# A transformer layer on one core: the order of the first batch's keys, values, norms and queries

## The chip, the core and the metric

The kernel runs on one core of a Trainium2 chip. A core has TensorE (PE in the rows; PEld is its loading of weights), VectorE (DVE), ScalarE (ACT), GpSimd (POOL), and SyncE (SP), which here issues most transfers. Each engine works through its own list of instructions in order; semaphores make one wait for another. The metric is the time of one execution on the device in microseconds (us), as the median of several runs; lower is better.

## The reference, cut to what matters

```python
# x: (16, 64, 512); ctx_1024: (16, 1601, 512); 16 heads of 32
def xattn(q, k, v, mask, w_q, w_k, w_v, w_o):
    query, key_, value = proj(q, w_q), proj(k, w_k), proj(v, w_v)      # (x @ w.T) by heads
    scores = einsum('bhqd,bhkd->bhqk', query, key_) / sqrt(32)
    scores = where(mask == 0, -1e9, scores)
    return merge(softmax(scores) @ value) @ w_o.T
x = x + xattn(layernorm(x), ctx_1024, ctx_1024, mask, w_q, w_k, w_v, w_o)
x = x + self_attention_with_lora(layernorm(x))
x = x + mixture_of_20_experts_top_2(layernorm(x))
```

The change concerns the beginning of the first line, the cross-attention.

## The kernel before

Context and keys. The kernel looks through the mask on the chip and finds which of five chunks of 400 context columns count; with these inputs one chunk does. So each of the 16 batches has 400 keys and values, which are computed from one piece of context of 128 x 4 x 400 numbers (800 KB; the 4 are slices `k` of the 512 features). Queries are computed once for all batches: 1024 rows of x, in two halves of 512 rows, four groups `m` of features each.

Precision. A matrix product of float32 data is made of three products (`mm3`, L186 to L190): each operand is split in a high part, copied by ACT to the type fp32r (`weight_hi`, `context`, `turn_x` in `scalar`), and a low part, source minus high part, by DVE (`rest`, L1084; `weight_lo`, `context`, `turn_x` in `vector`). A product can begin only when both parts of both operands are there. The helper line of every copy of ACT is L761, of every such subtraction L1084; of products L188 to L190, of transposes L194.

Stages. First the preamble, which the change reorders: load x in two halves, take its norms (`bn`, `variance`; POOL's `power` gives the inverse root), find the used chunks (`cm`, `fl`, `fr`, `frow`, `used`), normalise (`apply_x`, into `xn`, two buffers), transpose (`turn_x`, through banks 5 and 6 into `xt`, one buffer for both halves), queries (`queries(0)`, `queries(1)`, four products each), the keys of batch 0 (`k_part(0, g)`, four) and its values (`v_part(0, j)`, four). Then batches n = 0 to 15: `cross` writes each engine's order out by hand. For n it interleaves the transposes and value products of batch n - 1 (`t_part`, `pv_part`) with the keys of n (`k_part`), then scores (`s_part`, two halves) and values (`v_part`); DVE subtracts from the row's extreme, ACT exponentiates, POOL scales (L1637). Then the output projection, self-attention and the experts, which the change leaves as they are.

Order. PSUM banks 0 to 3 are given out in turn by the list `uses`; `freed` makes a product wait until the use four places before it has been read out. In the preamble PE's order is: transposes 0 to 3, two LoRA products, `queries(0)`, transposes 4 and 5, keys 0 and 1, transposes 6 and 7, keys 2 and 3, `queries(1)`; then `cross(0)` begins with scores and values of batch 0. SP issues in this order: constants, LoRA factors, first half of x, the mask rows (1 MB), the query weights `wq` (1 MB), the context of batch 0 once x is there, `wk` and the second half of x once the mask rows are there, mask and exclusions, and `wv` once DVE has split `wq` (both use `raw[:, 0]`). The next batch's context is issued when DVE has split the last one.

## Time and profile before

| | |
|---|---|
| time, median of 3 runs | 773.29 us (771.12 to 774.63) |
| span of the profiled execution | 772.6 us |
| busy share of the span | PE 92%, PEld 75%, DVE 53%, ACT 47%, POOL 37% |
| granted TensorE clock, mean | 0.960 of full speed |
| DMA | 74.77 MB |

The profile was taken in one execution. Of it the page gives the span, from the first instruction to the last, and no other time; the median of the runs is 0.7 us above this span. A busy share is an average over stages; the windows below tell them apart. In the page's second part the span is cut into 40 slices of 19.3 us, with the busy tenths of each. PE has 1 in the first slice and 9 in the next 30; DMA has 8 in the first slice, 4 in the second, and 0, 1 or 2 in the 29 after it.

### The profile page before, as it was taken

How to read it: one execution, taken by the hardware profiler on the slowest of the kernel's cores; microseconds unless marked ns; L12 is line 12 of the kernel's file. 1: busy time of each engine (PE TensorE's matmuls, PEld its weight loads, DVE VectorE, ACT ScalarE, POOL GpSimd, SP SyncE). 2: the span in 40 equal slices, each digit the busy share in tenths (PEclk: the TensorE clock that was granted, in tenths of full speed). 3: DMA queues.
4: the chain of work that ended last, by engine and by line, in shares of the span. 5: the costliest groups of instructions: out<-in, count | busy, mean ns of one | idle time of the engine just before them, and what ended most of it. 6: DMA issues, size and time to landing. Idle time of an engine off the chain costs nothing.

```text
span 772.6 us, 16928 instructions
## 1 busy us (share of the span) xinstructions
PE 708.0 (92%) x6817; PEld 581.6 (75%) x6817; DVE 410.2 (53%) x938; ACT 360.6 (47%) x665; POOL 289.0 (37%) x259
## 2 busy tenths in 40 slices
PE   1999999999999999999999999999999766999970
PEld 0787788778878887888788977887778554788860
DVE  5834434453344424533543345735368348799965
ACT  2425445453545345535454343533455431599950
POOL 0005135513553255225532453432225132788530
PEclk9999999999999999999999999999999985799995
DMA  8401101220021101110110002021001580999818
GB/s 294 149 1 43 45 2 45 98 91 24 29 98 44 44 2 44 44 39 7 44 44 2 3 3 75 1 79 45 3 29 57 188 303 21 330 394 397 333 52 326
DMA packets 30268, 74.77 MB, mean 97 GB/s; under 512 B 4053, under 2 KB 4437, under 8 KB 29155
## 3 DMA queue, kind: packets, MB, share of 16 engines
q1 hardware_dynamic: 25778, 65.16, 23.6%
q0 software_dynamic: 4400, 8.41, 2.9%
q8 instruction: 58, 0.95, 0.5%
q14 instruction: 32, 0.25, 0.1%
HBM read 66.13 MB, written 13.44 MB: 103 GB/s over the span
## 4 chain that ended last, share of the span: by engine, by line
PE 86%; DVE 6%; DMA 3%; ACT 2%; issue 2%; SPq 0%; POOL 0%; DVEq 0%; POOLq 0%; ACTq 0%
PE bank L188 22%; PE bank L190 21%; PE bank L189 20%; PE bank L194 10%; PE bank L345 4%; PE bank L322 3%; DMA raw<-in_wq 2%; DVE x_sb L1611 1%; PE bank L564 1%; DMA wr<-scratch_ys 1%; PE bank L551 1%; PE bank L665 1%; PE bank L580 1%; DVE wh L1084 1%; DVE stats L1340 0%
## 5 line engine op out<-in xcount | busy, mean ns | idle before, releaser
L1637 POOL TENSOR_SCALAR pp<-pp,rl 128x400 f32<-128x400 f32 x128 | 163.8, 1297 | 234.8 <-DVE rl L1162 234.8
L1217 DVE COPY pt<-bank 128x512 f32<-128x512 f32 x64 | 44.3, 692 | 99.4 <-PE bank L194 99.3
L188 PE MATMUL bank<-chi,wk 128*128 128x400 f32 x256 | 93.5, 365 | 0.0
L844 ACT ACTIVATE pp<-pp,acc 128x400 f32<-128x400 f32 x128 | 79.0, 619 | 28.0 <-DVE acc L1250 27.7
L1250 DVE CUSTOM_DVE_ANT_0 pp<-bank,cap 128x400 f32<-128x400 f32 x128 | 66.8, 569 | 46.5 <-PE bank L322 46.5
L190 PE MATMUL bank<-chi,wk 128*128 128x400 f32 x256 | 88.3, 345 | 0.0
L189 PE MATMUL bank<-clo,wk 128*128 128x400 f32 x256 | 88.3, 345 | 0.0
L188 PE MATMUL bank<-wv,chi 128*128 128x512 f32 x200 | 83.5, 417 | 0.0
L189 PE MATMUL bank<-wv,chi 128*128 128x512 f32 x200 | 78.5, 393 | 0.0
L190 PE MATMUL bank<-wv,clo 128*128 128x512 f32 x200 | 78.5, 392 | 0.0
L761 ACT ACTIVATE pt<-bank 128x512 f32<-128x512 f32 x64 | 38.2, 597 | 76.4 <-PE bank L194 75.3
L194 PE MATMUL bank<-cst,pp 128*128 128x128 f32 x512 | 67.2, 274 | 0.6 <-DVE x_sb L1194 0.6
L188 PE MATMUL bank<-wh,xu 128*128 128x512 f32 x152 | 65.8, 433 | 1.0 <-DVE xu L1084 0.7
L194 PEld LDWEIGHTS bank<-cst,pp 128*128 128x128 f32 x512 | 58.5, 140 | 5.8 <-issue 0.8
L190 PE MATMUL bank<-wh,xu 128*128 128x512 f32 x152 | 62.2, 409 | 0.0
L189 PE MATMUL bank<-wh,xu 128*128 128x512 f32 x152 | 61.8, 407 | 0.0
L761 ACT ACTIVATE vv<-bank 128x512 f32<-128x512 f32 x50 | 29.1, 583 | 65.0 <-PE bank L190 65.0
L188 PEld LDWEIGHTS bank<-wv,chi 128*128 128x128 f32 x200 | 37.5, 187 | 27.9 <-issue 19.4
L1149 DVE COPY kk<-bank 128x400 f32<-128x400 f32 x32 | 18.4, 575 | 61.9 <-PE bank L190 61.9
L189 PEld LDWEIGHTS bank<-clo,wk 128*128 128x128 f32 x256 | 48.3, 189 | 0.0
L188 PEld LDWEIGHTS bank<-chi,wk 128*128 128x128 f32 x256 | 48.2, 188 | 0.0
L190 PEld LDWEIGHTS bank<-chi,wk 128*128 128x128 f32 x256 | 48.1, 188 | 0.0
(238 smaller groups left out, 1387.4 us busy)
## 6 DMA issues: line engine op xcount, KB each, us to landing
wr<-in_We SPq DMA_DIRECT2D x13, 1024.0 KB, 11.6
craw<-in_ctx SPq DMA_DIRECT2D x16, 800.0 KB, 4.4
raw<-in_We SPq DMA_DIRECT2D x8, 1024.0 KB, 10.5
acc<-in_We SPq DMA_DIRECT2D x6, 1024.0 KB, 11.0
scratch_xn<-acc SPq DMA_DIRECT2D x16, 256.0 KB
wr<-scratch_ys SPq DMA_DIRECT2D x8, 512.0 KB, 7.2
x_sb<-in_x SPq DMA_DIRECT2D x2, 1024.0 KB, 8.5
out_dram<-x_sb SPq DMA_DIRECT2D x8, 256.0 KB, 5.9
```

Of the source, the lines that this page charges most:

```text
L188: pe.matmul(o, lhs[0], rhs[0], start=start, stop=False)
L189: pe.matmul(o, lhs[0], rhs[1], start=False, stop=False)
L190: return pe.matmul(o, lhs[1], rhs[0], start=False, stop=stop)
L194: last = pe.transpose(bank[0:n, k * 128:(k + 1) * 128], of(k), ident)
L322: last = pe.matmul(scores[64 * c:64 * c + 64, j, :], qc[r, 2 * half + c, 64 * b:64 * b + 64], kk[r, 2 * half + c, :], start=True, stop=True)
L345: last = pe.matmul(turned[32 * j:32 * j + 32, g, :], vv[:, (25 * (n // 8) + 3 * (n % 8) + i4) % 4, 128 * g + 32 * j:128 * g + 32 * j + 32] ...
L761: return act.activation(dst, src, ACT.Copy)
L844: act.activation(frame(p8), frame(p8), ACT.Exp, bias=bias, scale=-1.0, accum_out=total).then_inc(S["a_exp"], 1)
L1149: dve.tensor_copy(kk[:, g, :], at("k", 4 * n + g)[:, 0:CW]).then_inc(S["v_k"], 1)
L1217: dve.tensor_copy(pt[:, p8 % 4, :, :].rearrange("p a c -> p (a c)"), at("t", 8 * (n - 1) + p8)[:, :]).then_inc(S["v_pt"], 1)
L1250: dve.tensor_tensor_reduce(out=frame(p8), in0=scores[:, p8 % 4, :], in1=cap[:, :], scale=-1.0, scalar=nm[:, b, p8:p8 + 1] if seg else 3e38 ...
L1637: pool.tensor_scalar(frame(p8), frame(p8), rl[:, n % 2, p8:p8 + 1], None, ALU.mult).then_inc(S["g_pn"], 1)
```

## The change

The first context and `wk` are loaded in four pieces, one for each slice `k`, each with a semaphore of its own (`d_first`), ahead of everything but the constants; ACT and DVE split each piece as it comes (`first_keys`), and PE multiplies it for all four key groups, which stay open in banks 0 to 3. Then come three of the four values of batch 0, and only then the transposes of x and the queries, of which four are made between the scores of batch 0. `wq` now uses the slot of `wk`, is loaded when `wk` is split, and its low part is computed by POOL. All eight tiles of `xn` have their own place (in `acc`), and the second half of `xt` lies in `oh`, so the waits for a free buffer go. The LoRA products move to the start.

```diff
+        xn = acc[:, 0:8 * D].rearrange("p (i n) -> p i n", i=8)
...
-        xt = [sb(f"xt{j}", [128, 4, 512], f32r, first) for j in range(2)]
-        xn = sb("xn", [128, 2, D], f32, first)
+        xt = [[sb(f"xt{j}", [128, 4, 512], f32r, first) for j in range(2)], oh]
...
-        uses = [("q", m) for m in range(4)] + [("k", g) for g in range(4)] + [("q", 4 + m) for m in range(4)]
+        uses = [("k", g) for g in range(4)] + [("v", j) for j in range(3)] + [("q", m) for m in range(7)]
+        uses += [("v", 3), ("q", 7)]
...
+            def lora_products():
+                pe.wait_ge(S["d_cst"], 16)
+                pe.wait_ge(S["d_par"], 16)
+                for j in range(2):
+                    last = pe.matmul(pb[4][:, j * 128:(j + 1) * 128], lora[:, 2 * j, :], lora[:, 2 * j + 1, :],
+                                     start=True, stop=True)
+                last.then_inc(S["p_ids"], 1)
+
+            def first_keys():
+
+                c = columns(0)
+                for k in range(4):
+                    pe.wait_ge(S["v_w"], k + 1)
+                    for g in range(4):
+                        last = mm3(pe, at("k", g)[:, 0:CW], [w[:, k, g * 128:(g + 1) * 128] for w in wk],
+                                   [chi[:, k, c], clo[:, k, c]], k == 0, k == 3)
+                        if k == 3:
+                            last.then_inc(S["p_k"], 1)
+
+            def used_chunks():
+                pe.wait_ge(S["v_ids"], 3)
+                pe.transpose(pb[7][0:NC_, 0:128], fl[:, 0:NC_], ident).then_inc(S["p_ids"], 1)
+
+            def chunk_order():
+                pe.wait_ge(S["v_ids"], 4)
+                pe.matmul(pb[7][0:1, 0:10], fr[:, :], cst[0:NC_, 128:138], start=True, stop=True).then_inc(S["p_ids"], 1)
...
                 pe.wait_ge(S["v_xn"], i + 1)
-                if i >= 2:
-                    pe.wait_ge(S["v_xt"], i - 1)
-                turn4(pe, pb[5 + i % 2], lambda k: xn[:, i % 2, k * 128:(k + 1) * 128]).then_inc(S["p_xt"], 1)
-
-            def queries(hf):
-                pe.wait_ge(S["v_w"], 1)
+                if i >= 3:
+                    pe.wait_ge(S["v_xt"], i - 2)
+                elif i == 0:
+                    pe.wait_ge(S["v_ids"], 2)
+                turn4(pe, pb[4 + i % 3], lambda k: xn[:, i, k * 128:(k + 1) * 128]).then_inc(S["p_xt"], 1)
+
+            def queries(n):
+                hf, m = divmod(n, 4)
+                pe.wait_ge(S["g_h"], 1)
                 pe.wait_ge(S["v_xt"], 4 * hf + 4)
-                for m in range(4):
-                    for ready in freed("q", 4 * hf + m):
-                        pe.wait_ge(*ready)
-                    for k in range(4):
-                        last = mm3(pe, at("q", 4 * hf + m)[:, :], [w[:, k, m * 128:(m + 1) * 128] for w in wh[0]],
-                                   [v[:, k, :] for v in xt], k == 0, k == 3)
-                    last.then_inc(S["p_q"], 1)
+                for ready in freed("q", n):
+                    pe.wait_ge(*ready)
+                for k in range(4):
+                    last = mm3(pe, at("q", n)[:, :], [w[:, k, m * 128:(m + 1) * 128] for w in wh[0]],
+                               [v[:, k, :] for v in xt[hf]], k == 0, k == 3)
+                last.then_inc(S["p_q"], 1)
...
-                    if new:
...
+                    elif new:
+                        queries(4)
+                        s_part(0, 0)
+                        queries(5)
+                        s_part(0, 1)
+                        queries(6)
+                        v_part(0, 3)
+                        queries(7)
+
+            lora_products()
+            first_keys()
+            v_part(0, 0)
+            v_part(0, 1)
+            used_chunks()
+            for i in range(4):
+                turn_x(i)
+            v_part(0, 2)
+            chunk_order()
             queries(0)
-            turn_x(4)
-            turn_x(5)
-            k_part(0, 0)
-            k_part(0, 1)
-            turn_x(6)
+            queries(1)
+            for i in range(4, 7):
+                turn_x(i)
+            queries(2)
             turn_x(7)
-            k_part(0, 2)
-            k_part(0, 3)
-            queries(1)
-            pe.wait_ge(S["v_ids"], 5)
+            queries(3)
...
                 act.wait_ge(S["p_xt"], i + 1)
-                if i >= 4:
-                    act.wait_ge(S["p_q"], 4)
-                copy(xt[0][:, :, (i % 4) * 128:(i % 4 + 1) * 128], kview(pb[5 + i % 2])).then_inc(S["a_xt"], 1)
+                copy(xt[i // 4][0][:, :, (i % 4) * 128:(i % 4 + 1) * 128], kview(pb[4 + i % 3])).then_inc(S["a_xt"], 1)
+
+            def first_keys(k):
+                act.wait_ge(d_first[k], 32)
+                copy(chi[:, k, columns(0)], craw[:, k, :])
+                copy(wk[0][:, k, :], raw[:, 1, k, :]).then_inc(S["a_w"], 1)
+
+            def half_hi(dst, src, h):
+                copy(dst[0][:, 2 * h:2 * h + 2, :], src[:, 2 * h:2 * h + 2, :]).then_inc(S["a_w"], 1)
...
+            def value(n, j):
+                if j >= made(n + 1):
+                    return
+                act.wait_ge(S["p_v"], j + 1)
+                if n:
+                    act.wait_ge(S["p_pv"], 2 * n)
+                else:
+                    act.wait_ge(S["p_ids"], 1)
+                copy(vv[:, j % 4, :], at("v", j)[:, :]).then_inc(S["a_v"], 1)
...
                     for g in range(4):
-                        if g % 2 == 0:
-                            value(made(n) + g // 2)
+                        if not n:
+                            if g == 3:
+                                value(0, 3)
+                            else:
+                                queries(4 + g)
+                        elif g % 2 == 0:
+                            value(n, made(n) + g // 2)
...
+                    if n:
+                        value(n, made(n) + 2)
+                        value(n, made(n) + 3)
+                    else:
+                        queries(7)
...
-            weight_hi(wh[0], raw[:, 0], (d_raw[0], 16))
+            for k in range(4):
+                first_keys(k)
+            act.wait_ge(d_raw[0], 16)
+            half_hi(wv, raw[:, 0], 0)
+            half_hi(wv, raw[:, 0], 1)
+            k_part(0, 0)
+            k_part(0, 2)
+            act.wait_ge(d_raw[1], 16)
+            half_hi(wh[0], raw[:, 1], 0)
+            half_hi(wh[0], raw[:, 1], 1)
+            value(0, 0)
+            value(0, 1)
             for i in range(4):
                 turn_x(i)
-            context(0)
-            weight_hi(wk, raw[:, 1], (d_raw[1], 16))
-            weight_hi(wv, raw[:, 0], (d_raw[0], 32))
+            value(0, 2)
             queries(0)
+            context(1)
+            queries(1)
             turn_x(4)
             turn_x(5)
-            k_part(0, 0)
             turn_x(6)
+            queries(2)
             turn_x(7)
-            k_part(0, 2)
-            queries(1)
-            act.wait_ge(S["v_ids"], 5)
+            queries(3)
+            act.wait_ge(S["v_ids"], 7)
...
+            def first_keys(k):
+                dve.wait_ge(S["a_w"], k + 1)
+                c = columns(0)
+                ins = rest(clo[:, k, c], craw[:, k, :], chi[:, k, c])
+                if k == 3:
+                    ins.then_inc(S["v_ctx"], 1)
+                rest(wk[1][:, k, :], raw[:, 1, k, :], wk[0][:, k, :]).then_inc(S["v_w"], 1)
+
+            def first_values(h):
+                dve.wait_ge(S["a_w"], h + 5)
+                c = slice(2 * h, 2 * h + 2)
+                return rest(wv[1][:, c, :], raw[:, 0, c, :], wv[0][:, c, :])
...
-                if i >= 2:
-                    dve.wait_ge(S["p_xt"], i - 1)
-                norm(i, xn[:, i % 2, :]).then_inc(S["v_xn"], 1)
+                norm(i, xn[:, i, :]).then_inc(S["v_xn"], 1)
...
+                pv, c = kview(pb[4 + i % 3]), slice((i % 4) * 128, (i % 4 + 1) * 128)
+                rest(xt[i // 4][1][:, :, c], pv, xt[i // 4][0][:, :, c]).then_inc(S["v_xt"], 1)
...
-                    if b + 1 < NB:
+                        weight_lo(wh[0], raw[:, 0], 9)
+                    if n and b + 1 < NB:
                         context(n + 1)
...
-                            dve.wait_ge(S["p_q"], 8)
+                            dve.wait_ge(S["p_q"], 4)
...
-            dve.wait_ge(d_x[0], 16)
+            dve.wait_ge(S["p_ids"], 1)
+            for j in range(2):
+                own.on(dve.tensor_tensor(mbd[:, j, :], pb[4][:, j * 128:(j + 1) * 128], cst[:, 256:384], ALU.mult))
+            dve.wait_ge(own.sem, own.n)
+            for j in range(2):
+                dve.tensor_tensor(mbd[:, j, :], mbd[:, j, :], ident, ALU.add).then_inc(S["v_ids"], 1)
+            for k in range(4):
+                first_keys(k)
+            dve.wait_ge(S["d_x"], 16)
             for i in range(4):
                 own.on(bn(i))
             variance(0, 4)
+            first_values(0)
+            first_values(1).then_inc(S["v_w"], 1)
+            k_part(0, 1)
+            k_part(0, 3)
...
-            apply_x(0)
-            apply_x(1)
-            weight_lo(wh[0], raw[:, 0], 1)
-            dve.wait_ge(S["p_ids"], 1)
+            for i in range(4):
+                apply_x(i)
+            dve.wait_ge(S["p_ids"], 2)
             dve.tensor_reduce(fr[:, :], pb[7][0:NC_, 0:128], AX.X, ALU.max).then_inc(S["v_ids"], 1)
             for i in range(4):
                 turn_x(i)
-                if i < 2:
-                    apply_x(i + 2)
-                elif i == 2:
-                    dve.wait_ge(S["p_ids"], 2)
-                    dve.tensor_copy(frow[:, 0:10], pb[7][0:1, 0:10]).then_inc(S["v_ids"], 1)
-            context(0)
-            weight_lo(wk, raw[:, 1], 2)
-            dve.wait_ge(S["v_ids"], 3)
-            used()
-            dve.wait_ge(d_x[1], 16)
+            dve.wait_ge(S["d_x"], 32)
             for i in range(4, 8):
                 own.on(bn(i))
             variance(4, 4)
+            dve.wait_ge(S["p_ids"], 3)
+            dve.tensor_copy(frow[:, 0:10], pb[7][0:1, 0:10]).then_inc(S["v_ids"], 1)
             scaled(4, 4)
-            apply_x(4)
-            apply_x(5)
-            weight_lo(wv, raw[:, 0], 3)
+            for i in range(4, 8):
+                apply_x(i)
             make_cap(0)
-            dve.wait_ge(S["p_ids"], 3)
-            for j in range(2):
-                own.on(dve.tensor_tensor(mbd[:, j, :], pb[7][:, j * 128:(j + 1) * 128], cst[:, 256:384], ALU.mult))
-            dve.wait_ge(own.sem, own.n)
-            for j in range(2):
-                dve.tensor_tensor(mbd[:, j, :], mbd[:, j, :], ident, ALU.add).then_inc(S["v_lora"], 1)
-            turn_x(4)
-            apply_x(6)
-            turn_x(5)
-            apply_x(7)
-            k_part(0, 1)
-            turn_x(6)
-            turn_x(7)
-            k_part(0, 3)
             dve.wait_ge(S["v_ids"], 5)
+            used()
+            context(1)
+            for i in range(4, 8):
+                turn_x(i)
+            dve.wait_ge(S["v_ids"], 7)
...
+            for h in range(2):
+                pool.wait_ge(S["a_w"], 7 + h)
+                for k in (2 * h, 2 * h + 1):
+                    ins = pool.tensor_tensor(wh[0][1][:, k, :], raw[:, 1, k, :], wh[0][0][:, k, :].bitcast(f32),
+                                             ALU.subtract)
+            ins.then_inc(S["g_h"], 1)
             power(4, 4, (S["v_var"], 2), S["g_rstd"])
-            pool.wait_ge(S["p_q"], 8)
+            pool.wait_ge(S["p_q"], 4)
+            pool.wait_ge(S["v_xn"], 8)
+            pool.wait_ge(S["v_ids"], 7)
             alone(pool.memset(pp[:, 0:8 * D].rearrange("p (t c) -> p t c", t=8)[:, :, 0:PW], 0.0))
             alone(pool.memset(pp[:, 8 * D:8 * D + PW], 0.0))
...
+            for k in range(4):
+                sp.dma_start(craw[:, k, :], t["ctx"][0, 0, :, k, :]).then_inc(d_first[k], 16)
+                sp.dma_start(raw[:, 1, k, :], t["wk"][:, k, :]).then_inc(d_first[k], 16)
             xv = t["x"].rearrange("(i b) q d -> i (b q) d", b=2)
-            sp.dma_start(x_sb[:, 0:4, :], xv[0:4].rearrange("i p d -> p i d")).then_inc(d_x[0], 16)
+            sp.dma_start(x_sb[:, 0:4, :], xv[0:4].rearrange("i p d -> p i d")).then_inc(S["d_x"], 16)
+            sp.dma_start(raw[:, 0], t["wv"]).then_inc(d_raw[0], 16)
             for h in range(2):
                 sp.dma_start(mska[64 * h:64 * h + 64, :, :], t["rows"]).then_inc(S["d_cap"], 16)
-            sp.wait_ge(S["d_cst"], 16)
-            sp.dma_start(raw[:, 0], t["wq"]).then_inc(d_raw[0], 16)
-            sp.wait_ge(d_x[0], 16)
-            sp.dma_start(craw[:, :, :], t["ctx"][0, 0]).then_inc(S["d_ctx"], 16)
-            sp.wait_ge(S["d_cap"], 32)
-            sp.dma_start(raw[:, 1], t["wk"]).then_inc(d_raw[1], 16)
-            sp.dma_start(x_sb[:, 4:8, :], xv[4:8].rearrange("i p d -> p i d")).then_inc(d_x[1], 16)
+            sp.wait_ge(S["v_w"], 4)
+            sp.dma_start(raw[:, 1], t["wq"]).then_inc(d_raw[1], 16)
+            sp.wait_ge(S["d_x"], 16)
+            sp.dma_start(x_sb[:, 4:8, :], xv[4:8].rearrange("i p d -> p i d")).then_inc(S["d_x"], 16)
+            sp.wait_ge(S["v_ctx"], 1)
+            sp.dma_start(craw[:, :, :], t["ctx"][1, 0]).then_inc(S["d_ctx"], 16)
...
-                    context(16 * seg + b + 1, b + 1, chunk)
+                    if seg or b:
+                        context(16 * seg + b + 1, b + 1, chunk)
...
                     if seg == 0 and b == 5:
+                        sp.wait_ge(S["g_h"], 1)
...
+            sp.wait_ge(S["d_cap"], 32)
             for h in range(2):
                 sp.dma_start(mski[64 * h:64 * h + 64], t["mask"][0]).then_inc(S["d_cap"], 16)
             sp.dma_start(excl[:, :], t["excl"][0]).then_inc(S["d_cap"], 16)
-            sp.wait_ge(S["v_w"], 1)
-            sp.dma_start(raw[:, 0], t["wv"]).then_inc(d_raw[0], 16)
-            sp.wait_ge(S["v_ids"], 5)
+            sp.wait_ge(S["v_ids"], 7)
```

## Rows read from the trace of the kernel before

**Rows 1.** The chain that ended last, by engine (the page's part 4).

```profile
PE 86%; DVE 6%; DMA 3%; ACT 2%; issue 2%; SPq 0%; POOL 0%; DVEq 0%; POOLq 0%; ACTq 0%
```

**Rows 2.** Windows: us, busy time (count) by engine, TensorE clock, DMA share, GB/s.

```profile
24.50:72.40 47.90, 47.84 (x241) 39.02 (x241) 24.60 (x64) 20.38 (x38) 8.37 (x8) 1.00 0.11 37
...
175.00:470.00 295.00, 294.40 (x3246) 244.90 (x3245) 122.75 (x322) 130.75 (x297) 118.48 (x93) 1.00 0.09 30
```

**Rows 3.** Timeline of the start: start us, duration us, engine, line, out<-in.

```profile
9.01 0.69 DVE L1091 BATCH_NORM_STATS2 stats<-x_sb 128x6 f32<-128x512 f32 x1 [8.12 <-DMA x_sb<-in_x]
...
12.73 2.24 DVE L1270 TENSOR_REDUCE cm<-qc 128x5 f32<-128x2000 int32 x1 [0.23 <-DMA qc<-in_rows]
...
15.23 1.91 ACT L761 ACTIVATE wh<-raw 128x2048 fp32r<-128x2048 f32 x1 [13.20 <-DMA raw<-in_wq]
...
16.05 1.00 DVE L1100 TENSOR_SCALAR xn<-x_sb,mv,rstd 128x512 f32<-128x512 f32 x2
...
24.56 0.80 PE L188 MATMUL bank<-xt,wh 128*128 128x512 f32 x1
```

**Rows 4.** DMA issues of the first 6 us: KB, us from issue to landing.

```profile
vv<-in_lora SPq DMA_DIRECT2D x1, 32.0 KB, 2.3
```

**Rows 5.** Windows of the start; the last column is GB/s moved.

```profile
0.00:4.00 4.00, 0.00 (x0) 0.00 (x0) 0.06 (x1) 1.28 (x1) 0.33 (x5) 1.00 0.37 92
...
4.00:7.00 3.00, 0.00 (x0) 0.00 (x0) 0.00 (x0) 0.00 (x0) 0.00 (x0) 1.00 1.07 378
...
7.00:11.00 4.00, 0.00 (x0) 0.00 (x0) 1.93 (x5) 0.00 (x0) 0.00 (x0) 1.00 1.02 227
...
11.00:24.00 13.00, 5.26 (x21) 3.75 (x22) 11.29 (x23) 4.74 (x6) 1.05 (x1) 1.00 1.02 383
```

**Rows 6.** Groups on ACT and DVE, 0 to 72.4 us: busy us, mean ns.

```profile
L761 ACT ACTIVATE chi<-craw 128x1600 fp32r<-128x1600 f32 x2 | 3.0, 1525 | 0.0
...
L761 ACT ACTIVATE wk<-raw 128x2048 fp32r<-128x2048 f32 x1 | 1.9, 1904 | 0.0
...
L1084 DVE TENSOR_TENSOR clo<-craw,chi 128x1600 fp32r<-128x1600 f32 x2 | 3.6, 1822 | 0.7 <-ACT chi L761 0.7
...
L1084 DVE TENSOR_TENSOR wk<-raw,wk 128x2048 fp32r<-128x2048 f32 x1 | 2.3, 2291 | 0.0
...
L1084 DVE TENSOR_TENSOR xt<-bank,xt 128x512 fp32r<-128x512 f32 x8 | 5.4, 683 | 1.6 <-ACT xt L761 1.6
```

**Rows 7.** Timeline of PE's multiplications, early and at 660 us.

```profile
27.29 0.63 PE L188 MATMUL bank<-xt,wh 128*128 128x512 f32 x1
...
27.71 0.54 PE L189 MATMUL bank<-xt,wh 128*128 128x512 f32 x1
...
28.09 0.40 PE L190 MATMUL bank<-xt,wh 128*128 128x512 f32 x1
...
37.42 1.04 PE L194 MATMUL bank<-cst,xn 128*128 128x128 f32 x8
...
39.22 0.34 PE L190 MATMUL bank<-chi,wk 128*128 128x400 f32 x1
...
39.40 0.35 PE L188 MATMUL bank<-chi,wk 128*128 128x400 f32 x1
...
660.11 0.76 PE L188 MATMUL bank<-wh,xu 128*128 128x512 f32 x1 [0.65 <-DVE xu L1084]
...
666.49 0.40 PE L189 MATMUL bank<-wh,xu 128*128 128x512 f32 x1
```

**Rows 8.** Groups on POOL, whole span: busy us, mean ns.

```profile
L1684 POOL TENSOR_TENSOR x_sb<-x_sb,bro 128x512 f32<-128x512 f32 x8 | 12.3, 1534 | 0.5
...
L1700 POOL TENSOR_TENSOR wh<-raw,wh 128x512 fp32r<-128x512 f32 x4 | 5.1, 1296 | 0.0
```

**Rows 9.** Timeline of PE where batch 1 begins.

```profile
72.61 1.04 PE L194 MATMUL bank<-cst,pp 128*128 128x128 f32 x8
```

More of the change, by code:

```diff
@@ L176, in perceiver @@
         S = {n: sem(n) for n in names}
+        d_first = [sem(f"d_first{k}") for k in range(4)]
         d_we = [sem(f"d_we{i}") for i in range(R)]
@@ L232, in perceiver @@
                 n = 16 * seg + b
+                if n == 0:
+                    continue
                 for g in range(4):
@@ L261, in tensor @@
         def tensor(pe):
-            pe.wait_ge(S["d_cst"], 16)
-            pe.wait_ge(S["v_ids"], 1)
-            pe.transpose(pb[7][0:NC_, 0:128], fl[:, 0:NC_], ident).then_inc(S["p_ids"], 1)
+            def lora_products():
[5 more added lines that the diff above has]
+                last.then_inc(S["p_ids"], 1)
@@ L407, in cross @@
                         spread(n - 1)
-                    if new:
+                    if new and n:
                         for g in range(4):
@@ L471, in out_tile @@
                 if i % 2:
-                    pe.wait_ge(S["g_h"], i // 2 - 1)
+                    pe.wait_ge(S["g_h"], i // 2)
                 else:
@@ L785, in k_part, with queries @@
                 copy(kk[:, g, :], at("k", 4 * n + g)[:, 0:CW]).then_inc(S["a_k"], 1)
-            def queries(hf):
-                for m in range(4):
-                    act.wait_ge(S["p_q"], 4 * hf + m + 1)
-                    copy(qc[:, m, hf * 512:(hf + 1) * 512], at("q", 4 * hf + m)[:, :]).then_inc(S["a_q"], 1)
+            def queries(n):
+                hf, m = divmod(n, 4)
+                act.wait_ge(S["p_q"], n + 1)
+                copy(qc[:, m, hf * 512:(hf + 1) * 512], at("q", n)[:, :]).then_inc(S["a_q"], 1)
+            def value(n, j):
[7 more added lines that the diff above has]
+                copy(vv[:, j % 4, :], at("v", j)[:, :]).then_inc(S["a_v"], 1)
             def early_hi(i):
@@ L818, in cross @@
                         break
-                    if n + 1 < 16 * seg + NB:
+                    if n and n + 1 < 16 * seg + NB:
                         context(n + 1)
@@ L849, in cross @@
                                            ACT.Exp).then_inc(S["a_cor"], 1)
-                    value(made(n) + 2)
-                    value(made(n) + 3)
+                    if n:
[3 more added lines that the diff above has]
+                        queries(7)
                     if not seg and 0 <= n - SPLIT < EARLY:
```

58 lines of the change are left out of this document (16 added, 42 removed).

## The prediction

> **What bounds the kernel now.** I read the chain that ended last first: 86% of the span is PE's [rows 1]. The windows tell where: from 175 to 470 us PE is busy 294.40 of 295.00 us, and from 24.5 us to the end of batch 0's work 47.84 of 47.90 [rows 2]. So PE's work sets the time from its first dense product at 24.56 us [rows 3] on, and the kernel can win only what lies ahead of that, and must not open gaps behind it. The timeline shows what that first product waits for: the statistics of x start when x lands at 9.0, the mask's reduction when the mask rows land at 12.7, and ACT's split of the query weights when they land at 15.2; the first normalised rows start at 16.05, and transposes and their splits take the rest [rows 3]. Nothing of this is needed for keys and values. Batch 0's work ends at 72.4 us, and the first multiplication of a `t_part`, behind its weight load, is at 72.61 [rows 2, 9]; I compute when PE would get there after the change, and take the rest as shifted by the same amount, because contexts and weights are issued on events of the kernel itself and not at fixed times.
>
> **When the pieces land.** SP issues a transfer in some 0.4 us, faster than the bytes move. The start moves 92 GB/s x 4 us = 0.37 MB, then 378 GB/s to 7 us, 227 from 7 to 11 and 383 after [rows 5]. By the order of issue the slow stretch is the mask rows, which go to 64 partitions at a time; I take 380 elsewhere. Ahead of piece 0 stand the constants and factors, 0.23 MB; a piece is 0.205 + 0.262 = 0.467 MB. So the bytes of the pieces are moved at 0.37 MB + 0.38 MB/us: 4.9, 6.1, 7.3 and 8.6 us; x (1.05 MB) 11.3, `wv` 14.1, the rows (1.02 MB at 227) 18.6, `wq` 21.3, the second half of x 24.1, the next context 26.2. From the last byte to the landing: by the same sum x had been moved at 6.4 and landed at 9.0, `wq` at 13.5 and landed at 15.2, and a transfer of 32 KB took 2.3 us in all [rows 3, 4]. I take 2.0 (bounds 1.7 and 2.6): pieces 6.9, 8.1, 9.3, 10.6; x 13.3; `wv` 16.1; rows 20.6; `wq` 23.3; x 26.1; context 28.2.
>
> The Trainium skill, "DMA: Bandwidth & Descriptors" (Anatomy of one DMA, for transfers issued by GpSimd), fits about 2.0 us fixed per transfer plus bytes at 436 GB/s, which speaks against eight small ones. Added up, by that page's figures, eight would take 16 + 4.3 = 20 us (an estimate). That is a rival below, with a price from rows; the 378 GB/s with several transfers outstanding say that they overlap.
>
> **Splitting.** Durations scale with columns: ACT 1.525 us for 1600 and 1.904 for 2048 give 0.17 + 0.85 per 1000; DVE 1.822 and 2.291 give 0.15 + 1.05 per 1000 [rows 6]. A piece (400 + 512 columns) costs ACT 0.5 + 0.6 = 1.1 us, DVE 0.57 + 0.68 = 1.25. ACT is done with the pieces at 8.0, 9.2, 10.4, 11.7, DVE at 9.3, 10.5, 11.7, 13.0. PE starts at 9.3, 15.3 us earlier.
>
> **Keys.** Still 48 products of 400 columns. At 2.4 GHz they follow at 0.18 us (39.22, 39.40) [rows 7]. Before, the first dense products followed at 0.42 and went over to 0.24 near 27.9: some 3.3 us at 1.2 GHz, though the window's clock column says 1.00 there, so I go by the spacing. The other dense start, at 660.11, is slow until 666.49, 6.3 us [rows 7]. The new start comes out of a longer rest; I take 4.5 us: 13.5 products at 0.33 and 34.5 at 0.183, end 9.3 + 4.5 + 6.3 = 20.1. Pieces 1 to 3 (10.5, 11.7, 13.0) come before PE wants them (13.3, 16, 18), so PE is bound by itself. The longer low clock costs (4.5 - 3.3)/2 = 0.6 against before (bounds 0 and 1.5).
>
> **Values.** `wv` lands at 16.1, ACT's halves (1.04 each) end 17.2 and 18.2. DVE has meanwhile taken the statistics of four tiles (12.73 - 9.01 - 0.23 = 3.5) [rows 3], 13.3 to 16.8, and its halves (1.22 each) end 18.4 and 19.6. PE wants them at 20.1: cover 0.5 us. If x or `wv` is 1 us later, half of it is lost. Values 0 and 1 are 12 products of 0.233 each, 2.8 us: PE to 25.7.
>
> **Chunks, norms, transposes.** DVE reads out two keys to 20.8, then takes the mask's reduction to the first `xn` (12.73 to 16.05, 3.3) [rows 3]: 24.1, and four `xn` of 0.5 to 26.2. PE transposes tiles 0, 1, 2 to 27.1 (1.04 for two, of which 0.2 is the last one's tail: 0.44 each [rows 7]). Tile 3 needs bank 4 back, and so ACT: `wq` high 23.3 to 25.4, two values read out to 26.6, `xt` 0 to 27.2, then DVE's low part, 0.68 [rows 6], to 27.9. PE stands 0.85 us, is done at 28.4, and makes value 2 to 31.2.
>
> **Queries.** They need `wq`'s low part from POOL: four of 1.296 [rows 8], two behind each half of ACT's, 24.4 to 29.6. By POOL's slower group of this size, 1.534 [rows 8], it is 30.6. Both end before 31.4, so this costs nothing; the cover is 1.8 us, and `wq` later than 25.1 would cost one for one. The wait stands at the head of PE's queue, so everything would stand. The Trainium skill, "GPSIMD Engine Reference" (Specifications), says that POOL's SBUF interfaces are shared with VectorE; 1.296 against 1.534 may be that, and even the latter leaves the sum as it is.
>
> Queries 0 and 1 to 37.0. DVE meanwhile: four low parts of `xt` to 29.8, statistics to 33.3, POOL's power 1.0, four `xn` to 36.6, cap 0.9, the chunk list (eight small steps of 0.16) 38.8, the context of batch 1 (ACT has it at 36.6; landed 28.2) 2.0 to 40.8, then `xt` 4 at 41.5. PE: transposes 4 to 6 to 38.3, query 2 to 41.1, transpose 7 waits for that `xt` 4: 0.4 us lost, 42.0; query 3 to 44.8. The other `xt` are split at 43.4, ahead of query 4. Queries 4 to 7 11.2, two scores 2.4, value 3 2.8: 61.2 us. The scores' next half waits for four DVE passes of 0.5 under a query of 2.8; ACT's last exponential now stands behind value 3 at about 59.6, POOL's last scaling at 62.5, and the last transposes want it near 70.
>
> **Moved at no cost.** The LoRA products and their four small DVE steps run near 4 us, while every engine waits for piece 0. SP now holds mask and exclusions (0.4 MB) until the mask rows land at 20.6; they land near 29 and are wanted at 36.6. Behind SP's wait for the split of piece 3 (13.0) stand `wq`, x and the next context; by then the queue still holds `wv` and the rows, so the wait delays no byte. The next context after that is issued at 40.8 and not behind 60.
>
> **The sum.** 72.4 - 61.2 = 11.2 us. By parts: start 15.3; less four transposes that were in the wait before 1.8, the two chunk products 0.4, low clock 0.6, two stands 1.25. The query, key and value products are as many as before. 772.6 - 11.2 = 761.4 of span, and with the median 0.7 above the span 762.1.
>
> Bounds: clock 3.3 us, landing 1.7, no stands give 13.5, or 759.8; the executions differ by 1.7 to either side.
>
> **Rivals.**
>
> A. Late inputs. x, `wv` or `wq` land 3 to 6 us later than I sum (a back-pressured SP queue with twelve transfers outstanding, or 1600-byte runs that move like the mask rows at 227). The four pieces at 227 GB/s: 1.87 MB in 8.2 instead of 4.9 us, all behind it 3.3 later; PE is then late at `wv` by 2.8 and keeps it: 8.4 gained; with `wq` once more 2 us, 6. Time 765 to 767. For it: 227 is a rate of this very queue. Against: x in runs of 2 KB, right beside, moved at 378.
>
> B. Pieces one after another: each pays 2.3 us [rows 4], eight of them 18.4 + 4.9 of bytes: the last at 25, keys done at 25 + 1.1 + 1.25 + 2.2 = 29.6, 9.5 later, gain 1.7: 771.6. Or the change does not do what it says further on: an ordering of the new preamble (DVE's `xt` 4 behind the next context, ACT's exponentials behind queries) gives back 8 to 11 us. The cover against the latter is 5 us or more at each place but the two stands.
>
> C. Slower: the clock. PE is busy from 9.3 us, but with splits, evacuations and short transposes between, and if that keeps it at 1.2 GHz until the second query half the work of 24 us at full rate (9.3 to 33) takes 48: 12.8 more than the 11.2 gained: 774.9, and up to 778 if longer. It decides from 22 us of extra low clock on. For it: at 660 us the low level held 6.3 us of dense work after a broken stretch. Against: it did rise, and before it rose 3.3 us after 24.56 in the same preamble.
>
> **Numbers.** Forecast (8.5 to 13.5 gained) 0.72; A 0.13; B 0.08; C 0.05; 0.02 for what I don't see. A measurement of this kernel can tell about 0.5%, 3.9 us, from no change. Faster than that takes forecast, A and a little of B: 0.86; within it B's rest 0.08; slower 0.06. The range takes the forecast and most of A: 759 to 768.
>
> **What would show it.** PE's first key product near 9.3 us and 48 of them by 20; pieces landing about 1.2 us apart (A and B: more); no wait of PE on `wv`, under 1 us before transpose 3 and transpose 7, none at the first query on POOL; the first `t_part` near 61. The forecast is wrong if that first `t_part` comes at 64 or later, or if it comes early and the span does not follow.

## The result, and the profile after

The changed kernel took 766.74 us, median of 5 runs (765.24 to 769.05), against 774.63 (771.12 to 775.66) for the kernel before in the same session: a ratio of 0.9901, 95% interval 0.9881 to 0.9922. It is faster by 7.9 us; the forecast was 762.1, with a gain of 11.2, and the range of 759 to 768 holds the time. The profiled execution is the one with the median time; its span is 764.9 us against 772.6, so 7.7 us less.

The page of the changed kernel: its span, each engine's busy time and share, and the chain that ended last, by engine, which answers to [rows 1].

```profile
span 764.9 us, 16949 instructions
...
PE 708.5 (93%) x6817; PEld 582.0 (76%) x6817; DVE 411.2 (54%) x944; ACT 361.3 (47%) x673; POOL 296.9 (39%) x263
...
PE 84%; DVE 7%; DMA 3%; issue 2%; ACT 2%; SPq 1%; POOL 0%; DVEq 0%; POOLq 0%; ACTq 0%
```

Where batch 1 begins, PE's timeline of the changed kernel has (start, duration):

```profile
64.79 1.04 PE L194 MATMUL bank<-cst,pp 128*128 128x128 f32 x8
```

Before, this line stood at 72.61 [rows 9]. The 7.8 us between them are the whole gain of the span, 7.7. The same 295 us of the batches, moved forward by 7.8, follow in the windows of the changed kernel (stretch, length, then busy time and count of PE, PEld, DVE, ACT and POOL, granted clock, DMA share, GB/s), with the start in three parts:

```profile
8.77:26.50 17.73, 16.89 (x73) 15.32 (x74) 14.86 (x28) 7.87 (x12) 2.46 (x2) 1.00 1.04 337
26.50:35.60 9.10, 6.71 (x32) 5.09 (x30) 8.29 (x15) 2.85 (x5) 4.39 (x4) 0.81 0.32 92
35.60:64.70 29.10, 29.10 (x158) 22.32 (x157) 14.12 (x50) 13.97 (x31) 10.13 (x10) 1.00 0.09 29
167.20:462.20 295.00, 294.40 (x3246) 244.93 (x3245) 122.74 (x322) 130.75 (x297) 118.45 (x93) 1.00 0.09 30
```

PE's 294.40 us of 295 are those of before [rows 2]. What is lost lies between 26.5 and 35.6: PE busy 6.71 of 9.10 us, at a mean granted clock of 0.81. PE's waits of the changed kernel up to 70 us (line, releaser, us in total, times, longest):

```profile
PE bank L188 <- DVE wk L1136: 3.9, 1, 3.9
PE bank L270 <- DMA vv<-in_lora: 3.7, 1, 3.7
PE bank L194 <- DVE xt L1136: 1.6, 1, 1.6
PE bank L188 <- DVE wv L1136: 0.8, 1, 0.8
PE bank L194 <- DVE acc L1165: 0.8, 1, 0.8
```

The first two end when work begins; the other three, 3.2 us, are gaps in it. The timeline of the changed kernel around them (start, duration, engine, line, operation, out<-in, shapes, how many instructions the row takes together, and in brackets how long the engine had stood and what ended that):

```profile
8.77 0.70 PE L188 MATMUL bank<-chi,wk 128*128 128x400 f32 x1 [3.93 <-DVE wk L1136]
...
17.22 2.01 ACT L790 ACTIVATE wv<-raw 128x1024 fp32r<-128x1024 f32 x2 [5.56 <-DMA raw<-in_wv]
...
20.73 0.50 PE L188 MATMUL bank<-wv,chi 128*128 128x512 f32 x1 [0.84 <-DVE wv L1136]
...
24.95 4.82 DVE L1165 TENSOR_SCALAR acc<-x_sb,mv,rstd 128x512 f32<-128x512 f32 x4
...
25.08 5.80 POOL L1701 TENSOR_TENSOR wh<-raw,wh 128x512 fp32r<-128x512 f32 x4 [7.14 <-ACT wh L790]
...
28.41 0.65 PE L194 MATMUL bank<-cst,acc 128*128 128x128 f32 x4 [0.75 <-DVE acc L1165]
...
30.70 1.09 PE L194 MATMUL bank<-cst,acc 128*128 128x128 f32 x4 [1.64 <-DVE xt L1136]
...
35.64 0.50 PE L188 MATMUL bank<-xt,wh 128*128 128x512 f32 x1
```

PE's first key product is at 8.77 us, 15.8 before the first dense product of the kernel before [rows 3], and ahead of the 9.3 forecast. Then look at the two lines of 24.95 and 25.08. DVE's four normalisations take 4.82 us where two took 1.00 [rows 3], and beside them runs POOL's low part of `wq`, four of 1.45 us where they took 1.296 [rows 8]. DVE's `xt` subtractions, which free the banks of the transposes, stand behind those 4.82 us. Narrow windows of the same timeline take the row apart:

```profile
24.95 0.55 DVE L1165 TENSOR_SCALAR acc<-x_sb,mv,rstd 128x512 f32<-128x512 f32 x1
25.41 1.53 DVE L1165 TENSOR_SCALAR acc<-x_sb,mv,rstd 128x512 f32<-128x512 f32 x1
```

The first normalisation began before POOL did and took 0.55 us; the three behind it took 1.5 each.

### The profile page after: what moved, and what is told of

The parts are those of the page before. It is cut to its first block, busy times and chain, and to the rows that moved or that the text cites. A ratio compares the mean times of both kernels' runs of the same rounds, so it can differ in the third digit from the quotient of the medians.

```text
span 764.9 us, 16949 instructions
## 1 busy us (share of the span) xinstructions
PE 708.5 (93%) x6817; PEld 582.0 (76%) x6817; DVE 411.2 (54%) x944; ACT 361.3 (47%) x673; POOL 296.9 (39%) x263
## 4 chain that ended last, share of the span: by engine, by line
PE 84%; DVE 7%; DMA 3%; issue 2%; ACT 2%; SPq 1%; POOL 0%; DVEq 0%; POOLq 0%; ACTq 0%
PE bank L188 22%; PE bank L190 20%; PE bank L189 20%; PE bank L194 10%; PE bank L372 4%; PE bank L349 3%; DMA raw<-in_wv 1%; DVE x_sb L1668 1%; DMA wr<-scratch_ys 1%; PE bank L593 1%; PE bank L580 1%; PE bank L694 1%; PE bank L609 1%; DVE acc L1165 1%; DVE stats L1397 1%
## 6 DMA issues: line engine op xcount, KB each, us to landing
wr<-in_We SPq DMA_DIRECT2D x13, 1024.0 KB, 12.8
```

## The experiments

Two theories. T1: the missing microseconds are DVE and POOL standing in each other's way, the gap that this opens and the clock that falls after it; T2: they are late inputs (`wv`, mask rows, `wq`), because four pieces move slower than two whole loads. e1 to e4 ran on one chip, e0 and e5 to e7 on a second, e8 to e11 on a third, each group beside runs of the kernel before, with medians of 775.19, 774.27 and 774.61 us; a ratio is taken against these.

**e1_pool_late.** POOL begins when DVE has normalised the first four tiles.

```diff
+            pool.wait_ge(S["v_xn"], 4)
             for h in range(2):
```

> POOL's split of wq waits until DVE has written the first four xn. Theory (POOL's two-input subtractions slow DVE's normalisation, 4.82 us for four xn where the kernel before took 0.54 each): the four xn take about 2.0 us and end near 27.0 instead of 29.7, PE waits about 0.8 us ahead of transpose 3 and not 2.4 in all, its clock stays at 2.4 GHz, the low part of wq is ready at 32.4 to 32.9, the first query product starts near 32.7 instead of 35.6, and the span falls by 2.7 to 3.1 us, to about 762.0. Rival (the normalisation is slow for another reason, such as the transfers that still run or the new place of xn in acc): the four xn stay at 4.8 us, POOL starts at 29.8, and the span stays at 765 or rises by 1.

764.63 us (6 runs, 760.65 to 766.76), ratio 0.9845 [0.9815, 0.9875]. Its timeline:

```profile
18.74 2.00 ACT L790 ACTIVATE wv<-raw 128x1024 fp32r<-128x1024 f32 x2 [6.71 <-DMA raw<-in_wv]
...
26.54 1.92 DVE L1165 TENSOR_SCALAR acc<-x_sb,mv,rstd 128x512 f32<-128x512 f32 x4
...
28.54 5.00 POOL L1702 TENSOR_TENSOR wh<-raw,wh 128x512 fp32r<-128x512 f32 x4 [10.28 <-DVE acc L1165]
```

The four normalisations are back at 1.92 us, with `xn` still in `acc`, POOL's at 1.25 each, and the gap ahead of transpose 3 at 0.6. But in the profiled execution `wv` came 1.5 us later than in that of the changed kernel, PE stood 3.0 us for it, the first query came at 35.17 where I expected 32.7, and the span stayed at 765.0. The mechanism is shown, its worth not yet: the changed kernel was not run beside e1.

**e2_pool_busy_before.** The kernel before, with eight more POOL subtractions whose results nobody uses, from the inverse root on.

```diff
             power(0, 4, (S["v_var"], 1), S["g_rstd"])
+            for j in range(8):
+                pool.tensor_tensor(acc[:, j * D:(j + 1) * D], x_sb[:, j % 4, :], x_sb[:, (j + 1) % 4, :], ALU.subtract)
```

> The kernel before with eight subtractions of 128x512 added on POOL (x_sb minus x_sb into the still unused acc, results not used), from about 13.7 to 25 us. Theory (POOL against DVE): the two xn at 16 us, 1.00 us together before, take about 2.4 to 3.0 us; POOL's take 1.45 each and not 1.30. Open is which other DVE work is slowed: if every two-input DVE instruction from SBUF is, the split of wq (2.29 us) grows to 3 or more; if only the normalisation is, it stays at 2.3. PE's first dense product moves from 24.56 to between 25.5 and 28. Rival (place of xn or the transfers): xn stays at 0.5 each.

779.1 us, one run, span 777.3; the first dense product at 30.86 instead of 24.56, and later than the 25.5 to 28 that I expected. The mask rows came 1.3 us later (14.07 for 12.73), which is part of it. Its timeline:

```profile
13.41 10.20 POOL L1642 TENSOR_TENSOR acc<-x_sb 128x512 f32<-128x512 f32 x8
...
14.07 2.24 DVE L1270 TENSOR_REDUCE cm<-qc 128x5 f32<-128x2000 int32 x1 [1.78 <-DMA qc<-in_rows]
...
17.45 0.14 DVE L1277 TENSOR_SCALAR rows<-rows 128x1 f32<-128x1 f32 x1
...
18.30 1.31 DVE L1117 TENSOR_SCALAR rstd<-rstd,rows 128x4 f32<-128x4 f32 x1
19.64 2.85 DVE L1100 TENSOR_SCALAR xn<-x_sb,mv,rstd 128x512 f32<-128x512 f32 x2
...
22.41 3.35 DVE L1084 TENSOR_TENSOR wh<-raw,wh 128x2048 fp32r<-128x2048 f32 x1
```

So the effect is there without any of the change. A multiplication of four columns takes 1.31 us (0.22 in the changed kernel with POOL idle), about one POOL instruction (10.20 / 8 = 1.275); two normalisations 2.85 (1.00 before, [rows 3]), a little over one POOL instruction each; the split of `wq` 3.35 (2.29 for the same shape, [rows 6]), of which the 1.2 us until POOL's end at 23.61 brought next to nothing. The reduction, 2.24, costs what it did [rows 3].

**e3_fill.** PE multiplies nine products that nobody uses, three ahead of transpose 2 and six ahead of transpose 3; its gaps are filled, nothing else is earlier.

```diff
             for i in range(4):
+                if i == 2:
+                    pe.wait_ge(S["v_k"], 2)
+                for j in range((0, 0, 3, 6)[i]):
+                    pe.matmul(pb[3][:, :], tile_columns(chi, 0, 0), wv[0][:, 0, :], start=True, stop=True)
                 turn_x(i)
```

> Nine spare products of 128x512 (into bank 3, results not used) on PE in the two gaps ahead of transposes 2 and 3: 3 and 6 of them, 2.1 us. Theory (the gaps of 0.75 and 1.64 us let the clock fall to 1.2 GHz, and this costs half of the 3.3 us that follow): value 2 runs at 0.233 us per product throughout, the granted clock stays 1.00 at 31 to 34 us, the gaps end when they did, and the span falls by 1.2 to 1.6 us, to about 763.5. Rival (the slow products are slow because of what they read, next to POOL and the transfers): they stay at 0.43 and the span stays at 765 or rises by the part of the spare work that does not fit.

764.91 us (761.82 to 767.42), 0.9860 [0.9831, 0.9888]. The granted clock is 1.00 from 30 to 36 us, where the changed kernel's falls. But the profiled execution's first query (36.03) and span (765.0) are no earlier than the changed kernel's, where I expected a span of 763.5: the mask's reduction began 0.8 us later, and the four normalisations took 5.93 us for 4.82. The interval overlaps with that kernel's, so e10 repeats it beside it.

**e4_whole_load.** Context and `wk` in one transfer each; split and multiplied in four pieces still.

```diff
-                act.wait_ge(d_first[k], 32)
+                act.wait_ge(d_first[0], 32)
...
-            for k in range(4):
-                sp.dma_start(craw[:, k, :], t["ctx"][0, 0, :, k, :]).then_inc(d_first[k], 16)
-                sp.dma_start(raw[:, 1, k, :], t["wk"][:, k, :]).then_inc(d_first[k], 16)
+            sp.dma_start(craw[:, :, :], t["ctx"][0, 0]).then_inc(d_first[0], 16)
+            sp.dma_start(raw[:, 1], t["wk"]).then_inc(d_first[0], 16)
```

> The first context and wk are loaded by two whole transfers and not by eight; splitting and multiplying stay in four slices. Theory (what sets the time is the stretch from the mask rows and wq through norms and transposes, not the start): PE's first key product moves from 8.8 to about 13, keys end near 24 instead of 19.9, values 0 and 1 near 29.8, but transposes 2 and 3 come at 30 to 31.5 as before, without a gap that lets the clock fall; span within 1.5 us of 764.9 and more likely below. Rival (PE's start passes through to the end, as the prediction took it): span up by 3.5 to 4.2 us, to 768.5 to 769.

766.12 us (764.82 to 766.82), 0.9875 [0.9852, 0.9898]. PE begins at 11.65 instead of 8.77, yet batch 1 begins at 64.64. From 4 to 7 us 407 GB/s move, with the pieces 245:

```profile
4.00:7.00 3.00, 0.56 (x3) 0.26 (x2) 0.98 (x4) 0.00 (x0) 0.00 (x0) 1.00 1.01 407
```

and `wv` is there at 15.6, so PE doesn't wait for it. But `wq` too is earlier, POOL runs from 23.76 to 28.80, and now DVE's small steps and not its four normalisations (1.92 us) meet it. Timeline of this kernel:

```profile
23.76 5.04 POOL L1701 TENSOR_TENSOR wh<-raw,wh 128x512 fp32r<-128x512 f32 x4 [3.46 <-ACT wh L790]
...
25.41 0.94 DVE L1347 TENSOR_SCALAR cm<-cm 128x5 f32<-128x5 f32 x1
...
26.82 0.77 DVE L1354 TENSOR_SCALAR fl<-cm,rows 128x4 f32<-128x4 f32 x1
27.51 1.32 DVE L1182 TENSOR_SCALAR rstd<-rstd,rows 128x4 f32<-128x4 f32 x1
```

POOL's four instructions of 1.26 end near 25.0, 26.3, 27.5 and 28.8. The three of DVE end at 26.35, 27.59 and 28.83: each ends right behind one of POOL's. It is not a slowing by some factor but taking turns.

**e0_after** repeats the changed kernel beside e5 to e7.

> The changed kernel once more, beside the others on the same chip: 764 to 769 us, 0.988 to 0.992 of the kernel before. The landing of wv (17.2 us in its first profile) varies from execution to execution, and PE's wait for it with it (0.8 us there).

767.05 us (766.75 to 769.2), 0.9917 [0.9899, 0.9935]. PE waits 1.8 for `wv`, 1.6 and 0.3 at the transposes; batch 1 begins at 66.10. And the granted clock is low behind the first of these waits too, where the changed kernel's first profile, with a wait of 0.8, has 1.00 (window of e0):

```profile
24.00:25.00 1.00, 1.00 (x4) 0.80 (x3) 0.86 (x7) 0.97 (x2) 0.00 (x0) 0.50 1.07 396
```

**e5_wv_first.** `wv` is loaded ahead of x, and DVE splits it ahead of the statistics; POOL as in the changed kernel.

```diff
+            sp.dma_start(raw[:, 0], t["wv"]).then_inc(d_raw[0], 16)
             sp.dma_start(x_sb[:, 0:4, :], xv[0:4].rearrange("i p d -> p i d")).then_inc(S["d_x"], 16)
-            sp.dma_start(raw[:, 0], t["wv"]).then_inc(d_raw[0], 16)
...
+            first_values(0)
+            first_values(1).then_inc(S["v_w"], 1)
             dve.wait_ge(S["d_x"], 16)
...
             variance(0, 4)
-            first_values(0)
-            first_values(1).then_inc(S["v_w"], 1)
```

> wv is issued ahead of x, and DVE splits it ahead of the statistics; nothing else. Theory (after the change the path that ends last up to the first query is DVE's, from the mask rows through norms slowed by POOL, and not PE's): wv lands near 15 us, PE does not wait for it, but waits that much longer ahead of transposes 2 and 3; the first query product stays within 0.7 us of 35.6 and the span within 1 us of the changed kernel's. Rival (PE's waits add up one by one): the 0.8 us of that wait are gained, and more in executions where wv comes late.

767.41 us (764.8 to 768.67), 0.9910 [0.9890, 0.9929]: no gain over e0_after. The wait for `wv` is gone, but PE waits 2.3 us for normalised rows and 1.2 for `xt` instead, the granted clock is 0.50 to 0.53 from 28 to 36 us, and the first query comes at 38.91, against 36.95 in e0 and against the 35.6, give or take 0.7, that I expected. Late inputs alone (T2) are not it. One of e5's windows:

```profile
30.00:32.00 2.00, 1.48 (x6) 0.71 (x4) 2.00 (x3) 0.80 (x2) 1.72 (x2) 0.50 0.03 10
```

**e6_both.** e1's and e5's edits together.

> wv ahead of x, and POOL's split of wq waits for the first four xn. Theory (two waits, each of which hides what the removal of the other gives): no wait of PE on wv, four xn in 2.0 us, one wait of some 0.6 to 1.3 us ahead of the transposes and one of up to 1 us ahead of the first query, which starts near 32.4; span 761.5 to 762.5, 3 us below the changed kernel, with less spread than POOL's wait alone gave. Rival (the mask rows or wq land later and take it back): the first query at 34 or later, span 764 or more.

762.95 us (761.38 to 764.71), 0.9859 [0.9839, 0.9879], 4.1 us below e0_after's median, and the intervals are apart. PE's waits once it multiplies keys, then its timeline:

```profile
PE bank L194 <- DVE xt L1136: 0.7, 1, 0.7
PE bank L188 <- POOL wh L1702: 0.3, 1, 0.3
```

```profile
31.87 0.51 PE L188 MATMUL bank<-xt,wh 128*128 128x512 f32 x1 [0.31 <-POOL wh L1702]
...
61.05 1.04 PE L194 MATMUL bank<-cst,pp 128*128 128x128 f32 x8
```

With both causes away the first query and the start of batch 1 fall where the prediction had put them for the changed kernel (31.2 and 61.2).

**e7_whole_both.** e6 with e4's whole loads: are the pieces worth their place once nothing else is in the way?

> As wv first and POOL late together, but with the first context and wk in two whole transfers. It prices the four pieces where the later waits are short. Theory (most of PE's head start is spent in waits again): PE's first key product comes 3 us later (near 11.7), the first query only 0.5 to 1.5 us later, span 762 to 763.5. Rival (the head start passes through once the waits are gone): span 3 us above the version with pieces, about 765.

763.76 us (761.71 to 764.62), 0.9865 [0.9845, 0.9885]. PE begins 3 us later than in e6 and the first query is 1.5 later; the medians are 0.8 apart, which these runs can't tell from nothing.

**e8_warm_both.** e6 with three products that nobody uses ahead of the first keys, so that these run at 2.4 GHz from nearly the start.

```diff
             lora_products()
+            for j in range(3):
+                pe.matmul(pb[5][:, 0:384], ident, cst[:, 0:384], start=True, stop=True)
             first_keys()
```

> The version with both repairs (wv ahead of x, POOL after the first four xn) and three spare products of 128x384 float32 on PE between the LoRA products and the first key product (results not used), in time in which PE waited. Theory (with the repairs PE's path and the path mask rows, norms, wq low part end together at the first query, so more head start on PE buys nothing): the 48 key products run at 0.183 from near the start and end near 18 instead of 20.0, but transposes wait about 1.5 us more and the first query stays within 0.5 us of 31.9; span 0 to 0.6 us below the version without. Rival (PE's path alone sets it): 2 us below, near 757.5 of span.

762.31 us (759.3 to 763.58), 0.9832 [0.9812, 0.9851]. The first value product comes at 17.51 instead of 20.10, and PE gives it all back in five small waits of 0.4 to 1.0 us (e6 has 0.7 and 0.3): the first query comes at 32.09 for 31.87, batch 1 at 61.25 for 61.05. In these two traces what PE gains at the head no longer counts; the chain from mask rows over norms and the low part of `wq` sets the first query. The times can't confirm it: e6 and e8 ran on different chips, and e8 is 7.4 us below the changed kernel on its chip (e9), e6 4.1 below it on its own (e0). Both are faster than the kernel before and the changed kernel beside them.

**e9_after_again, e10_fill_again, e11_whole_again** run the changed kernel, e3 and e4 on one chip.

> The changed kernel, as the common base on this chip for the next two: 0.990 to 0.992 of the kernel before, 766 to 768 us.

> The spare products in the gaps of the changed kernel again, now beside the changed kernel. Theory (holding the clock is worth half of the slow 3.3 us): 1.0 to 1.6 us below the changed kernel. Rival (the first query is bound by DVE's chain and wq's low part, so value 2 at full clock only waits): within 0.4 us of it.

> The changed kernel with whole loads of the first context and wk, now beside the changed kernel. Theory: PE begins 3 us later, wv, mask rows and wq are not later than with the pieces, no gap is long enough for the clock to fall; 0 to 1.5 us below the changed kernel. Rival (the pieces' head start reaches the end): 3 us above it.

769.73 us (767.31 to 771.03), 0.9925 [0.9910, 0.9939]; 766.64 (764.63 to 767.69), 0.9889 [0.9872, 0.9906]; 767.63 (765.55 to 768.71), 0.9904 [0.9889, 0.9920]. In the profiled executions of e9 and e10 `wv`, the reduction and `wq` are equally late (within 0.2 us), and PE's first query comes at 38.75 and 36.89. PE's timeline, value 2 and the first query, in e9 and then in e10:

```profile
34.10 0.78 PE L188 MATMUL bank<-wv,chi 128*128 128x512 f32 x1
...
38.75 0.50 PE L188 MATMUL bank<-xt,wh 128*128 128x512 f32 x1
```

```profile
33.80 0.47 PE L188 MATMUL bank<-wv,chi 128*128 128x512 f32 x1
...
36.89 0.50 PE L188 MATMUL bank<-xt,wh 128*128 128x512 f32 x1
```

From the first product of value 2 it takes 4.65 us in e9 and 3.09 in e10: the clock is worth 1.6 of these 1.9 us. The medians are 3.1 apart, with intervals just apart, where I expected 1.0 to 1.6; the traces account for half of it. e11 against e9 is 2.1 us, the intervals overlapping: in the changed kernel no gain of the four small loads is shown.

e9 also prices e1. Their `wv` is equally late (19.00 and 18.74), and e1, with POOL behind the normalisations, has the first query at 35.17 for 38.75 and batch 1 at 64.64 for 67.90. So POOL's wait alone is worth some 3 us in the traces. Its median can't be set against e9's or e6's: e3 and e4, measured beside e1, have ratios 0.003 lower than their repetitions e10 and e11.

## Why the prediction was off by what it was

The range held the time, but the prediction had named a sign against itself: a first `t_part` at 64 us or later. It came at 64.79. The 766.74 us lie in the band of rival A (765 to 767), though in the profiled execution most of the loss is not A's; that the range held is in part luck. Of the other signs, PE waited 0.8 for `wv` (none forecast) and 2.4 at transposes 2 and 3 (under 1), and not at all at transpose 7 and for POOL.

Right: the place of the gain and what carries it. PE's start (8.77 for 9.3), the pieces' spacing (ACT begins them at 6.45, 8.19, 9.39 and 10.60; 1.2 to 1.7 us apart), 48 key products ending at 19.7 (20.1), a low clock of 4.5 us at their head (slow spacing from 8.77 to 13.27), and a batch loop that is only shifted. Rival B's transfers one after another did not come; the fixed 2.0 us a transfer of the Trainium skill's "DMA: Bandwidth & Descriptors" (Anatomy of one DMA) are not paid eight times over when eight are in flight, here by those 1.2 to 1.7 us a pair. Rival C's clock came in small, twice. C's price doesn't follow from its premise: 24 us of work at 1.2 GHz instead of 2.4 are 24 us more, 12.8 net of the gain, and that gives 786 us, not 774.9. Rival A came in part: `wv` 1.1 us late in this execution.

The forecast had the first query at 31.2 and batch 0's end at 61.2; they came at 35.6 and 64.7. The 4.4 us, stretch by stretch:

- Value 1 ends at 26.4 instead of 25.7: +0.7. PE starts 0.5 early, but the cover of 0.5 us on `wv` was too small. Over six profiled executions with `wv` behind pieces and x (the changed kernel's, e0, e1, e3, e9, e10), PE waited between 0.8 and 3.0 us. In the two with 0.8 and 1.2 us (the changed kernel's, e3) values 0 and 1 then took 5.7 us; in the four with 1.8 to 3.0 (e0, e1, e9, e10) the granted clock fell to 0.50 behind the wait, and they took 7.2. So in most executions this term is larger than in the one that this ledger is made from: in e9 value 1 ends at 29.7, 4.0 us after the forecast.
- Chunk product and four transposes take 5.0 us, to 31.4, where I had 2.7: +2.3. **This is the step that failed:** "Both end before 31.4, so this costs nothing". I had asked of POOL's split only whether it would be done in time. It was (30.9). What it costs is on the other side: four normalisations, 0.48 us apart with POOL idle (e1), take 4.82 in all, since three of them get through only behind a POOL instruction. They stand ahead of the `xt` subtractions in DVE's queue, the first of which frees the bank of transpose 3, so the stand of 0.85 became 0.75 + 1.64. That is 1.5 of the 2.3; the other 0.8 is in the transposes themselves, which no longer run one behind the other. I had even the rows for it: four `xn` against four POOL instructions of 1.296, one after another, is 5.2 us.
- Value 2 takes 4.2 us instead of 2.8: +1.4. Behind the gaps the granted clock fell to 0.50, as the windows of the changed kernel show:

```profile
30.00:31.00 1.00, 0.30 (x2) 0.33 (x3) 1.00 (x2) 0.00 (x0) 0.89 (x1) 0.72 0.00 0
31.00:32.00 1.00, 1.00 (x5) 0.92 (x4) 0.75 (x2) 0.17 (x1) 0.00 (x0) 0.50 0.00 0
...
33.00:34.00 1.00, 1.00 (x4) 0.79 (x3) 0.96 (x4) 0.00 (x0) 0.00 (x0) 0.57 0.00 0
34.00:35.00 1.00, 1.00 (x6) 0.80 (x5) 0.96 (x3) 0.00 (x0) 0.00 (x0) 1.00 0.03 8
```

That is 1.2 GHz until 33.7, products 0.43 apart instead of 0.23. I had priced each stand at its own length; here 1.4 us more followed behind stands of 2.4. e3 and e10, where PE has no such gap ahead of value 2, keep 1.00 there.

0.9 us comes back behind the first query: its 29.1 us are all busy, and the stand at transpose 7 did not come, since PE was late itself. 4.4 - 0.9 = 3.5, and that is the distance to the forecast in the span (764.9 against 761.4). The time missed by 4.6: the forecast added 0.7 us to its span, but each execution on record took 1.8 us longer than its own span (764.9 and 766.74 here), and that is the other 1.1.

The two causes overlap, but not evenly. With `wv` early alone PE comes sooner to transposes that are not ready, and e5 gains nothing; with POOL late alone the traces show 3 us (e1 against e9), and with both the medians show 4.1 (e6 against e0). How much of the 4.1 is due to `wv` was not measured, since e1 was not run beside e6. And the 15.8 us of head start were not all to be had: in the traces e8's first value product is 2.6 us earlier than e6's and batch 1 no earlier.

Open: why `wv` lands 1.6 to 4.1 us later behind eight small transfers than behind two whole ones (ACT begins on it at 17.22 to 19.20 in six executions against 15.15 and 15.63 in e11 and e4). The rate of 4 to 7 us differs, 215 to 286 against 407 and 415 GB/s; whether that is row length (1600 and 2048 bytes), the number of transfers or SP's issuing was not taken apart; e6 and e7, with `wv` right behind the first loads, can't tell, since in e7 ACT comes to it only at 13.07, when its own splits are done.

## What to carry to other kernels

Price work that you put on a free engine twice: when it ends, and what it does to the engine that takes turns with it. If DVE has short steps on the critical chain, let POOL's block of subtractions wait behind them; here one wait, with one load moved forward, was worth 4 us. Price a gap of PE at its length and, where the granted clock behind it falls, at the slow products too (here 1.4 us behind gaps of 2.4, and 1.5 behind waits of 1.8 to 3.0). A head start counts only as far as the next input on the longest chain is early as well.

## What the runs showed of the hardware

- DVE and POOL take turns, instruction by instruction. With a POOL `tensor_tensor` of two SBUF inputs (128x512, 1.26 to 1.45 us) running, these of DVE get through only when it ends: `tensor_scalar` on 128x512 (1.5 us instead of 0.55), on 128x4 and 128x5 (0.75 to 1.32 instead of about 0.2), and a subtraction of two SBUF inputs (3.35 instead of 2.29). These don't: reductions (2.24), a `tensor_scalar` of one column (0.14), and the subtraction from PSUM (three in 1.86 us in the changed kernel from 29.89, while POOL ran to 30.88; in e4, with POOL idle, 1.87). It goes the other way too: in e4 POOL's step of four columns took 1.95 us beside DVE's split of `wv`, 1.05 elsewhere. The Trainium skill, "GPSIMD Engine Reference" (Specifications), says that POOL's SBUF interfaces are shared with VectorE, with contention for DVE instructions in a 2-port mode or with two SBUF inputs. The traces agree for the subtractions: the one with two SBUF inputs meets POOL, the one from PSUM doesn't. Whether the `tensor_scalar` forms that meet it run in a 2-port mode no run here shows. That table has no price, and the price here is up to a whole POOL instruction for each of DVE's, however small. I had taken that rule for a price on POOL alone.
- The clock column can read 1.00 where products run at half rate: from 8.77 to 13.27 us they follow 0.33 us apart, later 0.18, and in e8, with other products ahead of them, 0.18 almost from the first on. In these runs the spacing is the better witness at the start.
- Eight transfers of 200 and 256 KB, several in flight at a time, moved 215 to 298 GB/s from 4 to 7 us (nine executions: the changed kernel's first, e0, e1, e3, e5, e6, e8, e9, e10), where two of 800 and 1024 KB moved 390 to 415 (e4, e7, e11).
